# A two-layer ViT tower on one core: GpSimd's bias parts, fills and two statistics moved, one image channel loaded ahead of the token constants

## The reference

```python
h = patch_embed(x, W) + b            # 32 images 3x96x96, patch 16 -> 36 tokens of 256
h = concat([cls_tok, cls_token, h]) + pos_embedding    # 38 tokens an image
h = h + attn0(layernorm(h))          # weights 1 + s + s*s/2, causal, divided by their sum + 1e-6
h = h + mxfp4_linear(layernorm(h))   # x_q @ w_q.T + bias; blocks of 32, scales 2^e * 2^(0.5*tanh(4*delta))
h = h + attn1(layernorm(h))          # softmax, causal, 16 heads of 16
h = h + ffn(layernorm(h))            # low rank 64, GELU, 1024 wide
```

## Time and profile before

| | us |
|---|---|
| median of 3 runs | 267.12 (265.94 to 267.68) |
| the profiled execution's own time | 265.32 |
| its span | 263.6 |
| PE busy in the span | 240.3 (91%) |
| DVE busy | 183.8 (70%) |
| POOL busy | 154.6 (59%) |
| ACT busy | 143.8 (55%) |
| granted TensorE clock, mean | 0.983 of 2.4 GHz |

### The profile page before, as it was taken

The page is one execution under the profiler, slowest core; times in us unless marked ns, Lnnn a source line. Parts: engine busy times, 40 slices in busy tenths (PEclk is TensorE's granted clock), DMA queues, the critical chain, the costliest instruction groups (busy, mean ns, idle before and its releaser), DMA issues.

```text
span 263.6 us, 7732 instructions
## 1 busy us (share of the span) xinstructions
PE 240.3 (91%) x3077; PEld 187.9 (71%) x3077; DVE 183.8 (70%) x348; ACT 143.8 (55%) x322; POOL 154.6 (59%) x234
## 2 busy tenths in 40 slices
PE   6897999883999899999999999699999998989992
PEld 6685888763888788887887888588888885434331
DVE  0435679311469999999999999998778886467021
ACT  3312114472798867877875645654656554833540
POOL 7541707887473967587789848946676661146000
PEclk9999999995999999999999999999999999999998
DMA  6989650000000000000001100010011011001021
GB/s 153 249 225 289 171 133 11 0 2 0 4 0 2 2 2 2 0 2 4 0 4 38 38 24 30 27 38 30 28 31 34 32 41 35 2 0 44 27 73 47
DMA packets 13081, 12.38 MB, mean 47 GB/s; under 512 B 4467, under 2 KB 12470, under 8 KB 13046
## 3 DMA queue, kind: packets, MB, share of 16 engines
q1 hardware_dynamic: 12618, 11.87, 16.2%
q10 hardware_dynamic: 428, 0.01, 0.1%
HBM read 8.07 MB, written 1.25 MB: 35 GB/s over the span
## 4 chain that ended last, share of the span: by engine, by line
PE 55%; DVE 27%; issue 6%; SPq 4%; DMA 4%; ACT 3%; DVEq 0%; ACTq 0%
PE psum L1389 9%; PE psum L1320 8%; PE psum L1558 4%; DMA img<-in_x 4%; DVE big L1075 4%; DVE img L1083 4%; PE psum L1711 3%; PE psum L1649 3%; PE psum L1699 3%; PE psum L1543 3%; PE psum L1435 3%; DVE st L1030 2%; PE psum L1623 2%; PE psum L1475 2%; PE psum L1451 2%
## 5 line engine op out<-in xcount | busy, mean ns | idle before, releaser
L1389 PE MATMUL psum<-hnT,a 128*128 128x114 f32 (+1 forms) x352 | 48.6, 281 | 0.2 <-ACT mT L732 0.2
L1389 PEld LDWEIGHTS psum<-hnT,a 128*128 128x128 f32 x352 | 43.5, 192 | 4.9 <-issue 1.7
L490 POOL TENSOR_SCALAR ve<-mvs 114x1 f32<-114x1 f32 x44 | 17.2, 390 | 44.5 <-DVE mvs L1032 42.5
L485 POOL TENSOR_SCALAR big<-mT,parmask 128x228 f32<-128x228 f32 x22 | 22.9, 1049 | 19.7 <-ACT mT L702 19.7
L1320 PE MATMUL psum<-wT,patchT 128*114 128x256 f32 (+1 forms) x132 | 30.1, 381 | 0.4 <-ACT patchT L637 0.4
L491 POOL TENSOR_TENSOR rstd<-ve,nhalf 114x1 f32<-114x1 f32 x44 | 26.8, 609 | 3.7
L1320 PEld LDWEIGHTS psum<-wT,patchT 128*114 128x114 f32 (+1 forms) x132 | 22.5, 175 | 5.6 <-issue 0.9
L511 POOL TENSOR_TENSOR big<-big,img 114x912 f32<-114x912 f32 (+1 forms) x11 | 21.8, 1984 | 6.8 <-ACT big L767 6.6
L1075 DVE SCALAR_TENSOR_TENSOR big<-big,img 114x912 f32<-114x912 f32 (+1 forms) x11 | 16.5, 1500 | 8.9 <-ACT big L756 8.9
L756 ACT ACTIVATE big<-psum 114x912 f32<-114x912 f32 (+1 forms) x22 | 18.8, 905 | 6.0 <-PE psum L1435 5.8
L1083 DVE RECIPROCAL img<-img 128x228 f32<-128x228 f32 x11 | 17.3, 1573 | 6.2 <-ACT img L773 6.0
(11 more groups left out here) (169 smaller groups left out, 561.8 us busy)
## 6 DMA issues: line engine op xcount, KB each, us to landing
img<-in_x SPq DMA_DIRECT2D x6, 576.0 KB, 9.6
img<-v_tok SPq DMA_DIRECT2D x66, 38.0 KB
out<-h_all SPq DMA_DIRECT2D x10, 114.0 KB
w_raw<-in_L_tok_W SPq DMA_DIRECT2D x3, 256.0 KB, 6.0
a_raw<-in_L_attn_Wq SPq DMA_DIRECT2D x1, 256.0 KB, 8.8
a_raw<-in_L_attn_Wk SPq DMA_DIRECT2D x1, 256.0 KB, 9.0
a_raw<-in_L_attn_Wv SPq DMA_DIRECT2D x1, 256.0 KB, 9.3
a_raw<-in_L_attn_Wo SPq DMA_DIRECT2D x1, 256.0 KB, 12.6
```

What stands on the lines that cost most here:

```text
L485: nc.gpsimd.tensor_scalar(mX[:, :, o, :], mT[:, :, :], parmask[:, o:o + 1], None, ALU.mult).then_inc(L["mX"], 1)
L1389: return nc.tensor.matmul(bk[:, m * T:m * T + TW[t]], w[:, c, m * 128:(m + 1) * 128], hnT[:, c, 0:TW[t]], start=(c == 0), stop=(c == DC - 1))
```

## The change

It moves work on three engines, and adds none but a second wait.

- SP issues the first channel of the images' second half, `load_channel(1, 0)`, right behind the three channels of the first half, so ahead of the six loads of `posb` and `tokb`. The load of `fbias` is now of 3 partitions instead of 114 and stands right behind those six, ahead of the other two channels of half 1.
- DVE takes `rfact` right behind the addition of `posb` and `tokb`, instead of inside `weight_scales`.
- GpSimd begins, after its constants, with `bias_parts`; then the statistics of tiles 0 to 4, the three fills, the statistics of tiles 5 to 8, and `layer0()`. The statistics of tiles 9 and 10 stand in `layer0()`, behind the mask of tile 1 (the mask issued in the loop's step t = 0).

```diff
@@ -140,7 +140,7 @@
-        fbias = sb("fbias", [T, D])
+        fbias = sb("fbias", [3, D])
@@ -347,6 +347,7 @@
                 load_channel(0, c)
+            load_channel(1, 0)
             sp.wait_ge(tok_zero, 1)
             for i in range(TI):
                 sp.dma_start(posb[i * S + 1:(i + 1) * S, :], dram["L0_tok_pos_embedding"][0, :, :]
@@ -354,13 +355,13 @@
-            for c in range(CH):
+            sp.dma_start(fbias[:, :], dram["L0_ffn_bias"].rearrange("(o n) -> o n", o=1).to_broadcast([3, D])
+                         ).then_inc(ld_b, 16)
+            for c in range(1, CH):
                 load_channel(1, c)
             for j, name in enumerate(["L0_attn_Wq", "L0_attn_Wk", "L0_attn_Wv", "L0_attn_Wo"]):
                 sp.dma_start(a_raw[:, j], dram[name].rearrange("(c p) n -> p c n", p=128)).then_inc(ld_a0, 16)
             sp.dma_start(qw[:, :, :], dram["L0_ffn_weight"].rearrange("(c p) n -> p c n", p=128)).then_inc(ld_qw, 16)
-            sp.dma_start(fbias[:, :], dram["L0_ffn_bias"].rearrange("(o n) -> o n", o=1).to_broadcast([T, D])
-                         ).then_inc(ld_b, 16)
@@ -497,6 +498,13 @@
+            def rstd_embedded(t):
+
+                pool.wait_ge(var_ready, t + 1)
+                step(static_rstd(t))
+                nc.gpsimd.tensor_scalar(shift[:, t:t + 1], mvs[:, t, 0:1], rstd[:, t:t + 1], -1.0, ALU.mult, ALU.mult
+                                        ).then_inc(shift_ready, 1)
@@ -550,6 +558,9 @@
                         mask_weights(t + 1)
                     if t == NT - 2:
                         round_to_grid((t - 3) // 2)
+                    if t == 0:
+                        for u in range(EARLY + WIDE, NT):
+                            rstd_embedded(u)
                     if t == 1:
                         weight_rest(2)
@@ -589,21 +600,18 @@
-            for t in range(NT):
-                if t == 7:
-                    pool.wait_ge(ld_b, 16)
-                    pool.wait_ge(rfact_ready, 1)
-                    bias_parts()
-                pool.wait_ge(var_ready, t + 1)
-                step(static_rstd(t))
-                nc.gpsimd.tensor_scalar(shift[:, t:t + 1], mvs[:, t, 0:1], rstd[:, t:t + 1], -1.0, ALU.mult, ALU.mult
-                                        ).then_inc(shift_ready, 1)
+            pool.wait_ge(ld_b, 16)
+            pool.wait_ge(rfact_ready, 1)
+            bias_parts()
+            for t in range(EARLY):
+                rstd_embedded(t)
             pool.wait_ge(by_patch_dve, 4)
             pool.wait_ge(by_patch_act, 2)
             nc.gpsimd.memset(pN, 0.0).then_inc(zeroed, 1)
             nc.gpsimd.memset(v_tok[:, :, :], 0.0).then_inc(zeroed, 1)
             nc.gpsimd.memset(img1[:, H * KEYS:H * KEYS + 2 * TI * H * HD], 0.0).then_inc(zeroed, 1)
-            pool.wait_ge(ld_b, 16)
+            for t in range(EARLY, EARLY + WIDE):
+                rstd_embedded(t)
             layer0()
             attention()
@@ -1003,7 +1011,6 @@
                 dve.wait_ge(factors, 2)
-                nc.vector.reciprocal(rfact[:, :], fact[:, :]).then_inc(rfact_ready, 1)
@@ -1023,6 +1030,8 @@
             dve.wait_ge(ld_tok, 16 * (2 + 2 * TI))
             step(nc.vector.tensor_tensor(posb[:, :], posb[:, :], tokb[:, :], ALU.add))
+            dve.wait_ge(factors, 2)
+            nc.vector.reciprocal(rfact[:, :], fact[:, :]).then_inc(rfact_ready, 1)
```

## The result

The changed kernel takes 257.39 us (median of 4, 257.26 to 258.99) against 267.16 for the kernel before (265.94 to 267.68): ratio 0.965, 95% interval 0.961 to 0.969. The forecast was 259.3 within 256.8 to 263.4. Its three terms came out as forecast; the medians moved 9.8 us apart instead of 7.84.

A forecast was written before the change was run, and what follows sets the result against it. PE, busy 91% of the span, was taken as the bound, with its gaps and clock to gain; 1.93 + 4.32 + 1.59 = 7.84 us off the median 267.12 gave 259.3 us, range 256.8 to 263.4.

The forecast's parts named there:

- The early gap: PE's idle time before channel (1, 0)'s patches, 21.66 to 23.59 us, goes with the earlier load: -1.93 us.
- Where the chain leaves PE: The chain of waits leaves PE twice before 64 us: for channel (1, 0)'s load and for POOL's mask.
- What is late next: Loads moved behind channel (1, 0) land later: constants at 22.56 (worst 25.3), channel (1, 1) at 24.4 to 25.7; no cost taken.
- POOL's order: PE's gap between the scores of tile 1 and the values of tile 0, 59.11 to 63.43, goes: -4.32 us.
- The first mask starts later than 55.3: Sign that the forecast is wrong, in POOL's timeline; the first mask was expected near 54.7 us.
- The clock: PE's half clock behind the gap before tile 0's values goes, the step from 8.21 to 6.62 us: -1.59 us.
- Rival A: PE's clock drops anyway near tile 0's values, 1.59 us of gain lost: 260.9 us; chance 0.10.
- The sum: At the kernel's end 7.84 us are gained: span 263.6 to 255.8, median 267.12 to 259.3.
- B: Early gain lost at PE's first gap, constants at 25.3 or channel (1, 0) at its old time: 261.2 us; chance 0.09.
- C: The gap before tile 0's values closes only half, masks late or ACT releasing the values: 261.5 us; chance 0.05.
- E: No measurable difference: SP's order does nothing and the mask finds another waiter, gain under 2.7, about 265.5 us; chance 0.03.
- D: POOL's queue head waits for `fbias`; PE's first transpose loses time if it lands after 27.1, about 270 at 38; chance 0.03.

The follow-up runs named there:

- e1: The kernel before with only the load of channel (1, 0) moved ahead of the small constants, GpSimd as before; 263.68 us, ratio 0.988.
- e4: The changed kernel with only the bias parts moved on GpSimd, all 11 statistics and then the fills in their old order; 257.41 us, ratio 0.965.
- e5: The changed kernel with the load of `fbias` put back behind that of `qw`; 259.33 us, ratio 0.972.
- e6: The kernel before with each position load of 37 rows issued as 32 and 5 rows, nothing moved; 263.73 us, ratio 0.988.
- e0: The changed kernel run again without an edit; 257.86 us, ratio 0.966 against the kernel before.
- e3: The kernel before with only the statistics of tiles 9 and 10 moved behind the mask of tile 1; 263.06 us, ratio 0.982.
- e10: The kernel of e3 run once more; 260.30 us, ratio 0.979 against the kernel before.
- e8: The changed kernel with each position load of 37 rows issued as 32 and 5 rows; 257.40 us, ratio 0.966.
- e9: The kernel of e4 with each position load of 37 rows issued as 32 and 5 rows; 257.39 us, ratio 0.966.
- e11: The kernel before run again without an edit, for its profile; 267.24 us.

## Why the prediction was right

- **The early gap, -1.93.** Right: from the embedding's start to the transposes' it was 23.59 - 18.71 = 4.88 us and is 21.86 - 19.07 = 2.79 in e1, 2.1 less, the idle time and 0.17 by which PE's records overlap. The channel landed later than my 14.8, 11.7 us after issue in e1, so near 16.4. The cover of 5.9 us took it.
- **Where the chain leaves PE.** The text says twice before 64 us. It left PE for ACT as well, at about 52, 54 and 57 us, with 0.78, 0.17 and 0.64 us of idle time; these waits are in the profiles after too, and no term of the sum hangs on them.
- **What is late next.** Right in kind. The constants were put at 22.56; DVE used them at 23.06 (e4) and 22.86 (e5) in executions that began like the profile of before, at 24.40 in the profile after, which began 1.76 us late. Channel (1, 1) landed at 24.6 to 25.5 there, within my 24.4 to 25.7. SP was held longer than I allowed: the last constant's issue ended at 15.4 (e4), 2.6 us later than before for a channel that I had put at 1.8.
- **The rule on how many engines a load uses.** By the rule of the Trainium skill ("DMA: Bandwidth & Descriptors", "Why a DMA increments its semaphore by 16 and not by 1"), the largest number up to 16 that divides the outer dimension, a load of 37 rows runs on one engine and one of 32 rows on 16. e6 fits it: SP's long issues before channel (1, 0), of which the earlier trace rows show one of 3.62 us, became 0.3. No trace here shows the engines one by one. The prediction used the rule for the slack only; that splitting the load closes the gap by itself it did not see.
- **POOL's order, -4.32.** Right, 4.3 to 4.4 (scores to values, start to start, 63.43 - 58.07 = 5.36 us before and 58.65 - 57.68 = 0.97 after). `bias_parts` took 9.11 us (25.17 to 34.28). The mask ended 58.65 - 58.28 = 0.37 us ahead of PE's values, forecast 0.5. POOL was ready for the mask 6.56 us ahead, not 3.9: a set of statistics takes 1.3 us, and the 1.6 of the prediction was a mean over four with one slow instruction among them (1.18 us for 0.22). What I did not see is that one of the three moves suffices (e4).
- **A sign of being wrong that did appear.** "The first mask starts later than 55.3": it started at 56.32 in the profile after, and at 55.67 in e0. Both executions began late, the first by 8.87 - 7.11 = 1.76 us, and counted from the first copy the mask is at 54.56, as forecast (54.7). The sign was set in absolute time, and the first channel's landing moves all of it.
- **The clock, -1.59.** Right: 6.62 instead of 8.21. Rival A was closer than its reasons: with a gap of 0.75 us the clock fell in e3 and held in e10. The changed kernel has no gap there, its clock held in both profiles, and the mean is 0.996 to 1.0 in all of its nine timed executions.
- **The sum.** 7.84 us against 263.6 - 255.7 = 7.9 in span (e8, e9; 255.8 in e4). As the median, 9.8. That 257.39 lies within the range is partly luck: the low end took the profiled base, 257.5, and another 0.64 of an idle time that stayed.
- **The step that was off** is the last one of the sum: "The median stands 1.8 above that execution; from the median 267.12 - 7.84". I took the distance between median and profile as noise that both kernels share. For the most part it is the half clock behind the early gap: at least 7 of the 21 executions of before with a clock on record have it, at most 10, and the profiled one had not (e11). The change removes that too, so the sum had to be taken from the profile (257.5) and the median's excess counted as a fourth term: at 24 to 28 us, (1.72 - 1.21) + (5.71 - 4.50) = 1.7 us when it happens. I had the sentence for it in hand, "the earlier idle of 1.93 us left the clock full", and took it from one execution for a property of the gap. The three times on hand (265.94, 267.12 and 267.68) already lay in the two groups.
- **Rivals B, C and E** didn't happen: both gaps closed whole. **D** was made to happen in e5 and left PE idle for 1.2 us with a landing at 29.9. By its threshold of 27.1 it would have been 29.9 - 27.1 = 2.8; but `bias_parts` took 8.8 us there and a set 1.3, where I had used the upper ends 10.1 and 1.6.

## What to carry to other kernels

One profile shows one execution: where its time differs from the median by more than the repeat of a kernel without gaps, look for a gap behind which the clock may or may not fall, and price it as a term that the change can remove. When a queue is late at a wait, list what stands in it ahead and when each input was ready; the single long block whose inputs are early (here the bias, 9.2 us) can be worth all the small moves together, and a load that a queue's head will wait for has to be issued early too. A small load of an awkward number of rows, here 37, can hold an issuing queue for microseconds: try to split it before reordering around it.

## What the runs showed of the hardware

- After the early gap PE's clock fell in some executions and not in others (2.19 and 1.85 us: fell; 1.93, 1.58 and 1.39: held), and after a gap of 0.75 us it did both, in one kernel. So the length of a gap alone didn't decide it. In e11 the granted clock was still full in the idle stretch (1.00 from 22 to 24 us) and fell when PE was back at work (0.64 from 24 to 26). The Trainium skill ("TensorE: Matmul & The Clock Gate", "Part 1: The HAM clock gate") says that the number of matmuls at the low clock varies from run to run, at the start of a kernel; the traces show a like variation at gaps within one.
- With three loads of 37 rows of 1 KB among them, two of the six small issues took 2.5 to 6.2 us each; with 32 and 5 rows each issue took 0.3 to 0.6.
- A single-input DVE instruction on SBUF (TENSOR_SCALAR, 128x512, 0.43 us) took 3.46 us while GpSimd's fills ran. Others beside such fills (the profile after, 41.3 to 44.4 us) kept their time: additions from PSUM 0.39, row statistics 0.43, two-input instructions of 128x512 on SBUF 0.66 and 0.69. One profile shows the long one; it was not tried by itself.
- The same first load landed 5.8 to 7.5 us after its issue, by the execution.
